# Attention's closing rows added by VectorE and stored plainly, with two parts of the next layernorm moved into attention's tail

## The reference

```python
x = x + _L0_gnn_ref(_layernorm(x), edge_index, W, a_left, a_right)   # attention, 8 heads of 32 channels
x = x + _L0_ffn_ref(_layernorm(x)[None], gate_w, gate_b, w1, w2, w3)[0]   # router, 2 of 16 experts
x = x + _L1_gnn_ref(_layernorm(x), edge_index, edge_attr_8, ...)     # three attention layers
x = x + _L1_ffn_ref(_layernorm(x)[None], ...)[0]

def _layernorm(x, eps=1e-05):
    m = mean(x, axis=-1); v = var(x, axis=-1)
    return (x - m) / sqrt(v + eps)

# in _L0_ffn_ref: logits = x @ gate_w + gate_b; probs = softmax(logits); top 2 of 16 per row
```

## Time and profile before

| | us |
|---|---|
| median of 3 runs | 3713.57 (3708.16 to 3714.67) |
| the profiled execution: its own time | 3700.15 |
| its span, first to last instruction | 3698.4 |
| attention phase, about | 447 to 1830 |
| layernorm and router logits (`node_phase`), about | 1830 to 1873 |
| router | 1873 to 1923 |
| experts | 1923 to 2300 |

### The profile page before, as it was taken

One profiled execution on the slowest core, in us unless ns is written; L12 is line 12 of the kernel. 1 busy time (PEld: TensorE's weight loads), 2 busy tenths in 40 slices (PEclk: granted clock), 3 DMA queues, 4 the chain that ended last, 5 costly groups with the idle time before them and its releaser, 6 DMA issues. The chain is left out here.

```text
span 3698.4 us, 69692 instructions
## 1 busy us (share of the span) xinstructions
PE 3390.1 (92%) x27261; PEld 2664.6 (72%) x27262; DVE 2779.2 (75%) x4220; ACT 2487.9 (67%) x4031; POOL 328.1 (9%) x281
## 2 busy tenths in 40 slices
PE   6999889999999999999569998899999999999999
PEld 4565566666666666666469997688878888888777
DVE  7999999999999999999452222765555654677594
ACT  5999899999999999999410110466656665676532
POOL 1000011010010010010104443000000000000000
PEclk9999999999999999999769999899999999999999
DMA  5434321121152121213568885322222221433101
GB/s 161 162 108 143 126 68 61 56 73 56 56 196 73 61 68 56 73 57 96 117 192 260 234 241 123 130 105 105 105 96 106 105 105 62 175 119 109 38 14 35
DMA packets 153157, 400.02 MB, mean 108 GB/s; under 512 B 27674, under 2 KB 99070, under 8 KB 134270
## 3 DMA queue, kind: packets, MB, share of 16 engines
q1 hardware_dynamic: 122120, 356.19, 28.0%
q0 software_dynamic: 27504, 36.13, 5.1%
q10 hardware_dynamic: 3206, 3.20, 0.4%
HBM read 337.50 MB, written 61.11 MB: 108 GB/s over the span
## 5 line engine op out<-in xcount | busy, mean ns | idle before, releaser
L963 ACT ACTIVATE hd_probsT<-hd_psT 128x768 f32<-128x768 f32 (+1 forms) x784 | 646.5, 851 | 70.5 <-PE hd_psT L1058 70.5
L1077 PE MATMUL hd_psO<-hd_probsT,hx 128*32 128x128 f32 (+2 forms) x10000 | 561.6, 279 | 135.0 <-ACT hd_probsT L963 135.0
L1597 PE MATMUL ly_psO<-hx_a,ly_probsT 128*128 128x256 f32 x2500 | 584.1, 381 | 0.0
L1077 PEld LDWEIGHTS hd_psO<-hd_probsT,hx 128*32 128x32 f32 (+1 forms) x10000 | 314.1, 108 | 324.2 <-ACT hd_probsT L963 219.7
L1546 ACT ACTIVATE ly_probsT<-ly_psT 128x768 f32<-128x768 f32 (+1 forms) x300 | 248.4, 828 | 392.7 <-PE ly_psT L1586 392.5
L1597 PEld LDWEIGHTS ly_psO<-hx_a,ly_probsT 128*128 128x128 f32 x2500 | 454.0, 189 | 71.4 <-issue 16.6
L1058 PE MATMUL hd_psT<-ident,hd_scores 128*128 128x128 f32 (+1 forms) x3250 | 469.0, 282 | 0.0
L1026 DVE CUSTOM_DVE_ANT_0 hd_scores<-hd_scores,mask_heads 128x3125 f32<-128x3125 f32 x130 | 443.4, 3410 | 5.5
L1022 DVE SCALAR_TENSOR_TENSOR hd_scores<-el_heads,hx 128x3125 f32<-128x3125 f32 x128 | 443.5, 3465 | 0.0
L954 ACT ACTIVATE hd_scores<-hd_scores,negmax 128x1664 f32<-128x1664 f32 (+1 forms) x260 | 420.1, 1616 | 13.5 <-DVE negmax L1026 13.4
L1058 PEld LDWEIGHTS hd_psT<-ident,hd_scores 128*128 128x128 f32 (+1 forms) x3250 | 348.2, 141 | 96.2 <-issue 95.7
(11 more groups left out here) (351 smaller groups left out, 5026.7 us busy)
## 6 DMA issues: line engine op xcount, KB each, us to landing
ly_mask<-mask_dram SPq DMA_DIRECT2D x72, 1568.0 KB, 6.7
moe_w<-in_L_ffn_w SPq DMA_DIRECT2D x144, 512.0 KB
mask_heads<-mask_dram SPq DMA_DIRECT2D x46, 1568.0 KB, 6.7
mask_dram<-el_heads SPq DMA_DIRECT2D x196, 196.0 KB, 1.9
el_heads<-el_dram SPq DMA_DIRECT2D x5, 1568.0 KB, 9.3
el_heads<-el_slope_dram SPq DMA_DIRECT2D x5, 1568.0 KB, 13.5
x<-x SPq DMA_DIRECT2D x8, 640.0 KB, 8.0
el_heads<-el_dram POOLq DMA_DIRECT2D x3, 1568.0 KB
```

The source lines that it names most:

```text
L963: nc.scalar.activation(pT[:, gi % 2, 0:w], psT[gi % 2][:, 0:w], ACT.Copy).then_inc(s_ev, 1)
L1077: last = nc.tensor.matmul(psO[B % 3][cg * CH:(cg + 1) * CH, h * P + d0:h * P + d0 + w], hx[0:r, tt, f0:f0 + CH], pT[0:r, gi % 2, t * P + d ...
L1597: last = nc.tensor.matmul(psO[B % 2][:, 0:D], pT[0:r, gi % 2, t * P:(t + 1) * P], hx[B // NB % 2][0:r, tt, 0:D], start=tt == 0, stop=tt == ...
```

## The change

In the attention phase:

- At its start SP first loads the 53 closing rows of `x1` into a tile `x_last`, by four transfers of 53 x 2 x 32 numbers, ahead of the loads of `el`.
- In the closing block SP waits until DVE has made the first unit's scores, which frees the first place of `el`, and then loads the first two parts of `x1` (ten blocks, `READY` = 2) into that room (`xr`).
- DVE, after the last unit's scores, takes the statistics of part 0, then the reciprocal of the closing block's sums as before, then the statistics of part 1. It waits for one square root of ACT over both parts, and normalises the ten blocks in place.
- ACT takes that root ahead of its copy of the closing sums.
- ACT writes the closing rows into `y_last`; DVE adds `x_last` in two instructions of 53 partitions; SP stores them by four plain transfers. The semaphore of these stores, `s_last`, is made outside the phase, so that the phase ends once they are issued. POOL issues none of them and waits for the 48 earlier stores only.

In `node_phase`, `done` = 2: three parts are loaded and normalised there, and PE starts on ten blocks that are ready. SP waits for `s_last` before it loads the closing rows. The rows are normalised in place, so `rn_x` and `rn_xn` are one tile.

For this the tile `el_heads` is kept over the whole program. The first block's rows, the experts' third weights, `y_last`, and later `hx_b`, `x3`, `xt`, `weights`, the projections `wx`, one of the three score tiles of `layers_phase`, its `xT` and its biases are views of it.

```diff
-               gelu=False, layernorm=True, x_tile=None, gate=None, s_kept=None):
+               gelu=False, layernorm=True, x_tile=None, gate=None, s_kept=None, done=0, s_last=None):
...
-                for p in range(NPART):
+                for p in range(done, NPART):
...
                         sp.wait_ge(s_pad, 2 if y_in is not None else 1)
+                        if s_last is not None:
+                            sp.wait_ge(s_last, 16 * 2 * PASSES)
                         sp.dma_start(x[0:EXTRA, FULL, :], x_in[FULL * P:N, :]).then_inc(s_in[p], 16)
...
-                for p in range(NPART):
-                    act.wait_ge(s_mv, p + 1)
+                for p in range(done):
+                    if p:
+                        copies(p - 1)
+                for p in range(done, NPART):
+                    act.wait_ge(s_mv, p + 1 - done)
...
-                    pe.wait_ge(s_n, b + 1)
+                    if b >= done * PART:
+                        pe.wait_ge(s_n, b + 1 - done * PART)
...
+        def closing_rows(q, e, kept):
+            x_rows = x1[FULLB * P:N, q * P:(q + 1) * P].rearrange("r (k e c) -> r k e c", e=2, c=CH)[:, :, e, :]
+            y_rows = kept[e * HALFP:e * HALFP + EXTRA, :].rearrange("p (k q c) -> p q k c", q=PASSES, c=CH)[:, q, :, :]
+            return x_rows, y_rows
+
         @block.sync
         def _(sp):
+            for q in range(PASSES):
+                for e in range(2):
+                    x_rows, y_rows = closing_rows(q, e, x_last)
+                    sp.dma_start(y_rows, x_rows).then_inc(s_xl, 16)
             load_el(sp, 0, HG - 1, 0)
...
+            sp.wait_ge(s_lk, LAST * HG + 1)
+            for i in range(3):
+                sp.wait_ge(s_store[i], 16 * len(range(i, FULLB + READY * PART, 3)))
+            for p in range(READY):
+                b0 = p * PART
+                sp.dma_start(xr[:, b0:b0 + PART, :],
+                             x1[b0 * P:(b0 + PART) * P, :].rearrange("(b p) f -> p b f", p=P)).then_inc(s_rows[p], 16)
+            sp.wait_ge(s_plus, 2)
+            for q in range(PASSES):
+                for e in range(2):
+                    x_rows, y_rows = closing_rows(q, e, y_last)
+                    sp.dma_start(x_rows, y_rows).then_inc(s_last, 16)
...
-            for q in range(PASSES):
-                rows_ = x1[FULLB * P:N, q * P:(q + 1) * P].rearrange("r (k e c) -> r k e c", e=2, c=CH)
-                for e in range(2):
-                    nc.gpsimd.dma_start(rows_[:, :, e, :], y[e * HALFP:e * HALFP + EXTRA, LAST % 3, :].rearrange(
-                        "p (k q c) -> p q k c", q=PASSES, c=CH)[:, q, :, :], accum_op=ALU.add).then_inc(s_store[LAST % 3], 16)
...
+                if B == LAST:
+                    act.wait_ge(s_lk, UNITS)
+                to = y[:, i, :] if B < LAST else y_last
...
+                    if gi == 3 and u + 1 == UNITS:
+                        act.wait_ge(s_mv, READY)
+                        nc.scalar.activation(rs[:, 1, :], rs[:, 0, :], ACT.Sqrt).then_inc(s_sq, 1)
...
+            for p in range(READY - 1):
+                deviation(p)
             sums(BLOCKS - 1)
+            deviation(READY - 1)
+            dve.wait_ge(s_sq, 1)
+            c(nc.vector.reciprocal(rs[:, 1, :], rs[:, 1, :]))
+            c.wait()
+            for b in range(READY * PART):
+                c(nc.vector.tensor_scalar(xr[:, b, :], xr[:, b, :], mv[:, b, 0:1], rs[:, 1, b:b + 1], ALU.subtract, ALU.mult))
+            c.wait()
+            dve.wait_ge(s_xl, 16 * 2 * PASSES)
+            dve.wait_ge(s_y, BLOCKS)
+            for e in range(2):
+                r = slice(e * HALFP, e * HALFP + EXTRA)
+                nc.vector.tensor_tensor(y_last[r, :], y_last[r, :], x_last[r, :], ALU.add).then_inc(s_plus, 1)
...
-        sc = sb("scores", [P, 3, N])
+        sc = [sb(f"scores{i}", [P, N]) for i in range(2)] + [room[:, 0:N]]
...
+    s_last = new_semaphore(nc, g, "rn_s_last_rows")
+    heads_phase(nc, g, *heads, s_last)
+    held.close()
```

More of the change, by code:

```diff
@@ L750, in normalise @@
                 part = slice(p * PART, (p + 1) * PART)
-                dve.wait_ge(s_sq, p + 1)
+                dve.wait_ge(s_sq, p + 1 - done)
                 step(nc.vector.reciprocal(rs[:, 1, part], rs[:, 1, part]))
@@ L759, in _ @@
                 nc.vector.memset(x[:, FULL, :], 0.0).then_inc(s_pad, 1)
-                add(0)
-                for p in range(NPART):
+                add(done)
+                for p in range(done, NPART):
                     stats(p)
@@ L822, with heads_phase @@
 CUT = T0[2] * P
+READY = 2
 assert sum(TG) * P >= N > (sum(TG) - 1) * P
 @phase
-def heads_phase(nc, g, hx, el, mask, sc_first, nm, x1):
+def heads_phase(nc, g, hx, el, mask, sc_first, nm, x1, xr, y_last, s_last):
     with ExitStack() as ctx:
@@ L852, in heads_phase @@
         s_er = sem("s_right_terms_of_pairs")
+        st = sb("st", [P, READY * PART, 6])
+        mv = sb("mv", [P, READY * PART, 2])
+        rs = sb("rs", [P, 2, READY * PART])
+        s_c, s_mv, s_sq = (sem(n) for n in ("s_c", "s_variance", "s_deviation"))
+        x_last = sb("x_of_last_rows", [P, P])
+        s_xl, s_plus = sem("s_x_of_last_rows"), sem("s_last_rows_plus_x")
+        s_rows = [sem(f"s_rows{p}") for p in range(READY)]
         block = ctx.enter_context(nc.Block())
@@ L1278, in layers_phase @@
 @phase
[L1279 removed]
+def layers_phase(nc, g, wx, hx, el, mask, y_last, x1, x, xt, wt, room, a):
     with ExitStack() as ctx:
@@ L2266, in program @@
         g["ident"] = sb("ident", [P, P])
+        tok = sb("slot_token", [P, NT], I32)
+        wgt = sb("slot_gate", [P, NT])
+        tile_e = sb("tile_expert", [1, NT], I32)
+        el = sb("el_heads", [P, HG, 2, NS])
+        places = el[:, :, :, :].rearrange("p h i n -> p (h i n)")
+        rows1 = places[:, 0:NB * D].rearrange("p (b d) -> p b d", d=D)
+        w3 = places[:, NB * D:NB * D + XE * HB * D].rearrange("p (e h d) -> p e h d", e=XE, h=HB)
+        wx_at = HG * 2 * NS - LAYERS * 2 * R1
+        wx = [places[:, n:n + 2 * R1].rearrange("p (k r) -> p k r", k=2)
+              for n in range(wx_at, wx_at + LAYERS * 2 * R1, 2 * R1)]
         with ExitStack() as s:
```

71 lines of the change are left out of this document (39 added, 32 removed).

## The result

The changed kernel takes 3682.12 us (median of six runs, 3674.74 to 3686.52), the kernel before 3707.01 (six runs, 3701.9 to 3714.67): ratio 0.9929, 95% interval 0.9908 to 0.995. The difference is 24.9 us; forecast were 22.9. The time is 0.9 us under the low end of the forecast's range: the three runs shown with the kernel before had a median of 3713.57, and with three more it is 3707.01. The first question is therefore whether the size of the difference was understood or only came out near.

A forecast was written before the change was run, and what follows sets the result against it. DVE bounds attention, a 21.2 us closing store and barrier follow, then PE bounds layernorm. Gains of 16.7 at the start and 7.7 in the phase, less 1.5 of stall: -22.9 us, median 3690.6, range 3683 to 3701.

The forecast's parts named there:

- the seam: Attention's end to the next phase: without POOL's accumulating stores the phase starts at 1814.1 against 1830.76, 16.7 us gained.
- Four loads ahead of `el`: Attention's start: four small loads delay those of `el`, DVE stalls 1.5 us, ends 0 and 7.7.
- b: Time one 53-row transfer keeps its way: taken as 0.9 us, between 0.5 and 2.4.
- The reload: Attention's tail: both parts of rows land by 1790, before DVE is free at 1794.39, so hidden with 4 us to spare.
- ACT and DVE: Attention's tail: table load and root delay ACT's rows 0.4 us to 1810.0; DVE sets the end at 1811.1.
- Stores and barrier: Attention's end: SP's four stores take 0.5 us each, POOL is off the path, next phase starts at 1814.1.
- Layernorm: Layernorm phase: PE starts at 1817.9 on weights and bias, works 30.0 us unbroken; the phase gives 7.7 us.
- The narrow way: Rival, 53-row transfers: carried as slowly as the accumulating ones, 2.4 us each; +11.1 us, 3701.7; chance 0.12.
- The interleaved loads: Rival, attention's tail: part loads share DMA engines with the reloads of `el`, DVE waits 6 us more, 3697; chance 0.05.
- the late stores: Rival, phase start: rows land after 1794.4 or the phase still waits for its stores, 2 to 10 us, near 3697; chance 0.04.
- The moved tile: Rival, later layers: the score tile's new address slows PE's 625 transposes; at 20% more, 3725 us; chance 0.04.
- The faster clock: Rival, layernorm phase: PE reaches 2.4 GHz, DVE becomes the bound, 9 us more gained, 3682; chance 0.07.

The follow-up runs named there:

- kernel d: Against the kernel before, only two parts reloaded and normalised in the tail, POOL still adding the closing rows into DRAM: 3695.1 us, ratio 0.9977.
- kernel a: Changed kernel with its four x loads of the last rows moved behind the eight small loads of the right terms: 3679.16 us, ratio 0.9928.
- kernel e: Against the kernel before, only the new placement of the tiles, with the old work in tail and layernorm: 3703.3 us, ratio 1.0004.

## Why the prediction missed by a little

**The step that failed is the level.** "The median of the three runs is 3713.57 ... I take the difference in time over to the median unchanged." Three runs spread over 6.5 us, the profiled execution lay 13.4 lower, and I laid the whole forecast on the higher number. Five medians of the kernel before are 3705.1 to 3707.1. With 3707.0 the same difference gives 3684.1, inside the range. So a level 6.6 us too high made most of the miss of 8.5 us. The range was mis-sized with it: it named 3 us for "the runs' own scatter", and the expert stage alone moves by 7 us between two profiles of one program. I had its length from one trace and wrote that all later phases would be of equal length, wrong beyond 2 us: that test says nothing on a stage that scatters more.

**The mechanism was right, its sum 2 us too high.** Of 22.9 forecast, the stages of two profiles show 20.8 and 20.6. The medians say 24.9 and 23.7, with intervals that span 18 to 34 us and hold both; whether the other 3 to 4 us are more than scatter stays open, so that the medians come so near to 22.9 may be luck. By stages the loads cost 1.4 us more than forecast and the seam gave 1.1 less, and the layernorm stage gave 0.7 more. Two of the forecast's own signs of being wrong came in: the next stage started at 1819.35 and not by 1816 (0.98 of it is a later start of attention, 2.94 the stall, 1.1 the seam), and a phase after the router changed by more than 2 us, by scatter as it proved. Term by term, in the forecast's order:

- *Four loads ahead of `el`:* 1.5 forecast, 2.94 measured, twice. The nearest rows gave 0.5 us an issue; four took 3.02, and the next load's issue took 1.69 instead of 0.32. I had a delay of 3.6 us by b; the second load of `el` was issued 4.4 us late and landed another 0.5 later, 4.9 in all, of which 1.9 were free. I also wrote 1.5 where my own terms gave 1.7. This is the largest miss of a size.
- *The reload:* hidden, right.
- *ACT and DVE:* table load on the path, 0.4 forecast; attention of kernel d, which has it on its path, is 0.4 longer than before. The forecast let ACT's four rows end at 1809.6, but the row's 0.82 us is for all four, so they ended at 1809.12; no term hangs on it. In the changed kernel PE's product behind the root took 1.74 instead of about 1.1 us (granted clock 0.80 from 1811 to 1812, then 0.50), and ACT ended 0.5 us ahead of DVE's normalising; in kernel a it was 1.1, and DVE set the end in both, as forecast. The drain that the Trainium skill ("ScalarE: Activation LUTs", What ACT_TABLE_LOAD costs) counts beside the table load, 2.66 us for both, is not seen: the root starts 1.30 us after the load of 1.28 began.
- *Stores and barrier:* 2.0 us forecast, 3.08 measured; from there to the next stage 0.96 forecast, 1.16 measured. Start of the closing block to the next stage: 15.6 gained, 16.7 forecast. "POOL is off the path" was wrong by its reason: its wait for ACT's last rows was still in the stream, and the drain behind it took 4.19 us, not 2.5. In the changed kernel SP's four issues just cover it.
- *Layernorm:* 3.8 us to PE's start forecast, 3.5 measured; 30.0 us of PE's work forecast, 29.7 measured; 7.7 gained forecast, 8.4 measured.

**The rivals.** The narrow way is half right: b is about 1.1, near my 0.9 and far from the rival's 2.4. The share of 0.09 to 0.10 while the stores move alone, where one engine of 16 would be 0.06, does speak for a narrow way, as by the rule of the Trainium skill that I cited ("DMA: Bandwidth & Descriptors", Why a DMA increments its semaphore by 16 and not by 1), but it did not bring that rival's price. The interleaved loads and the late stores did not come. The moved tile is excluded by kernel e. The faster clock came in no run without added work.

## What to carry to other kernels

Forecast the difference, and the absolute time from every level that is shown: where the median of a few runs and the profiled execution lie 13 us apart, the range has to hold both. When an engine's last work in a stage is taken away, take its last wait away too: its drain starts behind it and becomes a limit as soon as another goes. At such a seam every microsecond won uncovers the next wait (issue, drain, weights, a root ahead of copies), so move the small loads that the next stage begins with ahead of the last stores.

## What the runs showed of the hardware

- POOL's drain took 2.52 us behind its four accumulating stores (three traces) and 4.19 us where its stream ended with waits and none of those stores (eleven traces), whether or not it waited for ACT's last rows. What makes the difference is not shown.
- Small strided loads (53 rows, pieces of 128 bytes) issued by SP first took 3.02 us for four; behind the loads of `el` and the eight right terms they took 7.84 us, and by POOL 7.42. Four such stores, alone on the DMA engines, moved 11 to 13 GB/s, about 1.1 us each (an estimate).
- The granted clock rose to 1.00 in the layernorm stage after added transposes and fell again near 1833.9, with PE busy 9.08 of the 9.60 us before 1833.6. In the changed kernel it stayed at 0.50 through 29.7 us of PE work without a gap.
- The same program's expert stage took 383.3 or 390.2 us. Its length goes with how often POOL waits for its accumulating transfer.
